# Attention scores by 32-row float32 products and a pass through DRAM, in place of split products with pre-mixed queries

## What is computed

```
x  -> group norm -> q, k (256 channels), v4 (1024 channels), each a 1x1 convolution with scale and shift
vl = 3x3 depthwise convolution of v4, scaled and shifted
attn[h,i,j] = SCALE * sum_d q[h,i,d] k[h,j,d] + ab[h, offset(i,j)]
attn = einsum('hij,gh->gij', attn, th1w) + th1b      # heads mixed
attn = softmax(attn over j)
attn = einsum('hij,gh->gij', attn, th2w) + th2b      # heads mixed again
out  = x + conv1x1(relu(attn @ v + vl))
```

## Time and profile before

| what | value |
|---|---|
| median of three runs | 4534.46 us (4534.35 to 4535.85) |
| the profiled execution's own time | 4534.58 us |
| its span, first to last instruction | 4532.8 us |
| TensorE, VectorE, ScalarE, GpSimd busy | 99%, 93%, 79%, 30% |
| granted TensorE clock, mean | 0.999 of full |
| one steady round | 70.27 us |
| DMA engines busy, mean | 27.3%, 356 MB in all |

### The profile page before, as it was taken

The page is one execution under the profiler, slowest core; times in us unless marked ns, Lnnn a source line. Parts: engine busy times, 40 slices in busy tenths (PEclk is TensorE's granted clock), DMA queues, the critical chain, the costliest instruction groups (busy, mean ns, idle before and its releaser), DMA issues.

```text
span 4532.8 us, 108461 instructions
## 1 busy us (share of the span) xinstructions
PE 4505.5 (99%) x33666; PEld 4502.5 (99%) x33666; DVE 4197.4 (93%) x10015; ACT 3570.3 (79%) x8508; POOL 1360.9 (30%) x1288
## 2 busy tenths in 40 slices
PE   7999999999999999999999999999999999999999
PEld 7999999999999999999999999999999999999999
DVE  8999999999999999999999999999999999999998
ACT  7787877878778787787787877878778778787786
POOL 2323323323233232332322323323233232332322
PEclk9999999999999999999999999999999999999999
DMA  3322222223222232222322322223222232232222
GB/s 94 97 65 81 86 69 87 65 81 92 70 81 74 72 97 65 81 82 68 93 65 81 88 72 82 68 78 97 65 81 79 67 97 65 81 86 68 88 65 76
DMA packets 211502, 356.05 MB, mean 79 GB/s; under 512 B 15843, under 2 KB 132691, under 8 KB 211413
## 3 DMA queue, kind: packets, MB, share of 16 engines
q1 hardware_dynamic: 211478, 355.75, 27.3%
HBM read 199.71 MB, written 155.98 MB: 78 GB/s over the span
## 4 chain that ended last, share of the span: by engine, by line
PE 99%; DMA 0%; POOL 0%; DVE 0%; SPq 0%; ACT 0%; issue 0%; POOLq 0%; DVEq 0%
PE psA L293 45%; PE psA L426 15%; PE psL L293 13%; PE psM L293 10%; PE psM L404 9%; PE psL L404 7%; PE psA L306 0%; DMA qa<-in_wqkv 0%; SPq L254 0%; POOL xs L822 0%; DVE probs L730 0%; DMA by_key<-probs 0%; POOL wp_lo L863 0%; DVE q_lo L722 0%; ACT w_hi L443 0%
## 5 line engine op out<-in xcount | busy, mean ns | idle before, releaser
L700 DVE SCALAR_TENSOR_TENSOR psC<-vpad,par,psC 128x406 f32<-128x406 f32 x3072 | 1807.2, 635 | 0.0
L584 ACT ACTIVATE probs<-probs,nmax 112x196 f32<-112x196 f32 x1792 | 803.2, 451 | 128.8 <-DVE nmax L759 112.9
L293 PE MATMUL psA<-x_hi,w_lo 128*128 128x392 f32 x2304 | 794.9, 345 | 6.0 <-DVE x_lo L679 6.0
L293 PE MATMUL psA<-x_hi,w_hi 128*128 128x392 f32 x2304 | 785.7, 341 | 0.0
L293 PE MATMUL psA<-x_lo,w_hi 128*128 128x392 f32 x2304 | 785.1, 341 | 0.0
L426 PE MATMUL psA<-qa,shared 105*128 105x196 f32 x4096 | 690.9, 329 | 0.0
L426 PEld LDWEIGHTS psA<-qa,shared 105*128 105x128 f32 x4096 | 677.2, 190 | 0.4 <-DVE shared L794 0.3
L857 POOL TENSOR_TENSOR k_lo<-qk,k_hi 128x392 fp32r<-128x392 f32 x128 | 159.9, 1249 | 1636.4 <-ACT k_hi L490 1636.4
L722 DVE SCALAR_TENSOR_TENSOR q_lo<-qk,th,q_hi 128x392 fp32r<-128x392 f32 x1024 | 618.3, 632 | 2.0 <-ACT q_hi L486 1.9
L486 ACT ACTIVATE q_hi<-qk,th 128x392 fp32r<-128x392 f32 x1024 | 594.5, 618 | 2.1
L461 ACT ACTIVATE o_hi<-shared 128x392 fp32r<-128x392 f32 x512 | 271.6, 530 | 391.3 <-DVE shared L794 391.3
(11 more groups left out here) (85 smaller groups left out, 10723.1 us busy)
## 6 DMA issues: line engine op xcount, KB each, us to landing
by_key<-probs SPq DMA_DIRECT2D x512, 224.0 KB, 3.6
qa<-by_key SPq DMA_DIRECT2D x128, 448.0 KB, 4.3
qk<-by_key SPq DMA_DIRECT2D x128, 448.0 KB, 6.9
xs<-in_x SPq DMA_DIRECT2D x64, 588.0 KB, 3.8
shared<-in_x SPq DMA_DIRECT2D x64, 588.0 KB, 3.8
out<-shared SPq DMA_DIRECT2D x63, 588.0 KB, 3.0
qa<-in_wqkv SPq DMA_DIRECT2D x3, 768.0 KB, 7.1
stage_wp<-in_wp SPq DMA_DIRECT2D x1, 1536.0 KB, 9.6
```

What stands on the lines that cost most here:

```text
L293: last = nc.tensor.matmul(dst, w, r, start=(begin and n == 0), stop=(end and n == 2))
L584: nc.scalar.activation(row, row, ACT.Exp, bias=nmax[:, img, b:b + 1], scale=-1.0, accum_out=rowsum[:, img, b:b + 1]).then_inc(s_exp, 1)
L700: nc.vector.scalar_tensor_tensor(a if tap == 7 else sums, src, taps[:, c, TAPS[tap]:TAPS[tap] + 1], a if tap == 0 else sums, MUL, ADD).the ...
```

## The change

Scores are made per head, unmixed, from unsplit q and k, go through DRAM, and the heads are mixed by one matmul with a Kronecker product of th1 and the identity (`kron1`) as the stationary operand.

- **q and k** stay plain float32. SCALE is folded into the scale and shift of q (setup). q's columns are stored (column w, row b) in each image. The high and low halves of q and k, `th1`, k's split on GpSimd and the tensors for them are gone.
- **TensorE, behind value tile 3**: `head_scores`, four units (image 0 or 1; the first 112 or the last 84 queries). A unit is 8 matmuls, for two halves kt of the heads and four row tiles r, on 32 partitions each; tile r has a PSUM bank of its own out of psL and psM.
- **Copies**: ScalarE copies banks 0 and 1 of each unit, VectorE banks 2 and 3, into `scores` (part of `qa`). Each unit but the first waits for all four copies of the one before.
- **SyncE**: 8 stores of the scores to `head_rows` (two per unit, 784 B runs), then one load per image into `by_head` (112 partitions (head, column), 14 x 196 numbers each, part of `shared`), all ahead of the stores of turned values. The turned values' loads now wait for their stores alone. The row of ones is loaded once.
- **TensorE, logits**: behind projection 0, now 14 matmuls of 392 columns, one per two query rows. Projection 1 moves behind the logits.
- **VectorE**: 16 convolution steps, score copies, 8 steps, the turns (after three units' stores have landed), 4 steps, the 28 score rows with no convolution steps between them, then 18 steps before the second reciprocal.
- **ScalarE**: q and k right behind each other; value tiles 4 to 7 behind the score copies; the output of projection 1 is taken between exponentials 20 and 21.

```diff
+            def head_scores(t, first):
+                pe.wait_ge(s_qk_sb, 4 * t + 4)
+                for u, (img, c) in enumerate(UNITS):
+                    if u:
+                        pe.wait_ge(s_score_a, 8 * t + 2 * u)
+                        pe.wait_ge(s_score_v, 8 * t + 2 * u)
+                    elif not first:
+                        pe.wait_ge(s_mix_sb, 14 * t)
+                    at_ = img * PIX + c * WIDE
+                    for kt in range(QT):
+                        for r in range(QUADS):
+                            part_ = slice(r * KD, (r + 1) * KD)
+                            mm = nc.tensor.matmul(score_bank(r)[0:score_rows(c), kt * PIX:(kt + 1) * PIX],
+                                                  q[part_, kt, at_:at_ + score_rows(c)],
+                                                  k[part_, kt, img * PIX:(img + 1) * PIX], start=True, stop=True)
+                    mm.then_inc(s_score_mm, 1)
...
+                    if m == 3:
+                        head_scores(t, first)
...
                     project(t, 0, True)
-                    project(t, 1, True)
-                pe.wait_ge(s_klo, 2 * (t + 1))
-                pe.wait_ge(s_qlo, 16 * (t + 1))
                 for n in range(RES):
                     img, b0 = n // 7, 2 * (n % 7)
+                    if n % 7 == 0:
+                        pe.wait_ge(s_heads[img], 16 * (t + 1))
                     if n >= 4:
                         pe.wait_ge(s_score, 28 * t + 2 * n - 6)
...
+                    nc.tensor.matmul(logit_bank(n)[:, 0:2 * PIX], kron1[:, :, :].rearrange("p g i -> p (g i)"),
+                                     by_head[:, img, b0 * PIX:(b0 + 2) * PIX], start=True, stop=True
+                                     ).then_inc(s_logit_mm, 1)
...
+                    project(t, 1, True)
...
+            def score_copy(t, u, r):
+                img, c = UNITS[u]
+                act.wait_ge(s_score_mm, 4 * t + u + 1)
+                nc.scalar.copy(scores[0:score_rows(c), img, c, r:NH:QUADS, :],
+                               score_bank(r)[0:score_rows(c), :].rearrange("p (k n) -> p k n", k=QT)
+                               ).then_inc(s_score_a, 1)
...
+            def scores_out(t, u):
+                img, c = UNITS[u]
+                sp.wait_ge(s_score_a, 8 * t + 2 * u + 2)
+                sp.wait_ge(s_score_v, 8 * t + 2 * u + 2)
+                rows = head_rows[img].rearrange("h i j -> i h j")
+                middle = 4 * 16 if c == 0 else REST - REST % 16
+                parts = [(0, middle), (middle, score_rows(c))]
+                for lo, hi in parts:
+                    sp.dma_start(rows[c * WIDE + lo:c * WIDE + hi], scores[lo:hi, img, c, :, :]
+                                 ).then_inc(s_score_out[u], 16)
...
-                convs(6)
-                for _ in range(8):
-                    mixed_low(1)
-                    convs(1)
...
+                convs(16)
+                score_copies()
+                convs(8)
+                for u in range(3):
+                    dve.wait_ge(s_score_out[u], 32 * (t + 1))
                 turn(0)
...
                 turn(1)
...
-                convs(6)
+                convs(4)
                 for n in range(RES):
...
-                    convs(1)
-                convs(3)
+                convs(18)
```

More of the change, by code:

```diff
@@ L231, in _ @@
                 sp.dma_start(stage_w[:, :, cols], w_rows[:, :, cols]).then_inc(s_w[n], 16)
-            for dst, src in ((par[:, :], A["par"]), (th1[:, :, :], A["th1"]), (small[:, :], A["small"]),
+            for dst, src in ((par[:, :], A["par"]), (small[:, :], A["small"]),
                              (abx[:, :], A["abx"]),
@@ L274, in step @@
                     load_x(t + 1)
+                for u in range(4):
+                    scores_out(t, u)
+                if first:
+                    sp.wait_ge(s_bias, 1)
+                else:
+                    sp.wait_ge(s_olo, 8 * t)
+                    wait_alone(sp, s_av_mm, 8 * t)
+                heads_in(t, 0)
+                heads_in(t, 1)
                 turned_out(t)
-                ones_in(t)
                 keys_in(t)
@@ L390, in step @@
                 if not first:
+                    if not last:
+                        pe.wait_ge(s_gs, t + 2)
+                    project(t, 1, True)
+                if not first:
                     project(t, 2, True)
-                pe.wait_ge(s_ones_in, 16 * (t + 2))
+                if first:
+                    pe.wait_ge(s_ones_in, 16)
                 for use, (img, n) in enumerate(USES):
@@ L532, in step @@
                 conv_centre(t, 1)
+                if not first:
+                    act.wait_ge(s_vt_sb, 4 * t)
+                query_or_key(0)
+                query_or_key(1)
+                query_or_key(2)
+                query_or_key(3)
+                values(2)
+                values(3)
                 if first:
@@ L590, in step @@
                         conv_centre(t, CENTRES[n])
+                    if n == 20 and not first:
+                        projected(t, 1)
                 if not first:
@@ L595, in step @@
                     act.wait_ge(s_mix_mm, 14 * t + use + 1)
-                    if use == 0 and not first:
-                        act.wait_ge(s_av_mm, 8 * t)
+                    if use == 0:
+                        act.wait_ge(s_vt_out, OUTS * (t + 1))
                     if use == 7:
@@ L714, in step, with score_copies @@
                     dve.wait_ge(s_av_mm, 8 * t)
[L715 to L723 removed]
+                def score_copies():
+                    if first:
+                        dve.wait_ge(s_wlo, CT)
+                    else:
+                        dve.wait_ge(s_vt_sb, 4 * t)
+                    for u, (img, c) in enumerate(UNITS):
+                        dve.wait_ge(s_score_mm, 4 * t + u + 1)
+                        for r in (2, 3):
+                            nc.vector.tensor_copy(scores[0:score_rows(c), img, c, r:NH:QUADS, :],
+                                                  score_bank(r)[0:score_rows(c), :].rearrange("p (k n) -> p k n", k=QT)
+                                                  ).then_inc(s_score_v, 1)
                 def turn(half):
@@ L854, in step @@
             def step(t, first, last):
-                for kt in range(QT):
-                    wait_alone(pool, s_khi, 2 * t + kt + 1)
-                    nc.gpsimd.tensor_tensor(k_lo[:, kt, :], k[:, kt, :], k_hi[:, kt, :].bitcast(f32),
-                                            SUB).then_inc(s_klo, 1)
                 if first:
```

149 lines of the change are left out of this document (47 added, 102 removed).

## The result

The changed kernel takes 5054.52 us (median of four runs, 5048.46 to 5068.05), the kernel before 4535.01 on the same chip: a ratio of 1.115, with a 95% interval of 1.1124 to 1.1175. It is slower by 520 us. The forecast said slower by 296 (4830, range 4600 to 5150): the direction and the range held, the point was 225 us low. The profiled execution took 5059.76.

A forecast was written before the change was run, and what follows sets the result against it. TensorE was taken to bound the kernel end to end. A round: 12.85 + 10.6 + 10.7 + 9.45 + 8.6 + 10.75 + 10.63 + 1.3 = 74.9 us against 70.27, over 64 rounds 296 more: 4830 us, range 4600 to 5150.

The forecast's parts named there:

- What bounds the kernel before; slower, since each wait of TensorE is added in full: Whole round: TensorE's instructions set its 70.27 us, any TensorE wait adds in full; slower had chance 0.93.
- Scores, 10.6 us: Four score units on TensorE: three turns of 3.05 us plus 1.5, in place of nothing.
- the 1.5 us of passes in a unit: TensorE's 16 score passes per unit: 1.5 us taken, between 0.66 (four tiles at once) and 2.66 (one after the other).
- the first rival: Score units: row tiles overlap fully, units 0.66, turns about 2.3, scores 7.7, round 72.0, 4646 us; chance 0.2.
- VectorE's copies, forecast at 1.06: Between score units: two copies of 392-column banks, 0.49 + 0.57 = 1.06 us, with 1.3 as the upper case.
- Through DRAM, "I cost them at nothing": Score stores and head-row loads: both images' rows land just before TensorE asks, 0.5 to 1 us in hand, no cost.
- VectorE, a stall of 1.3 at the value product: Value product's third group, nominally at 42.15, waits for VectorE's first addition, done at 43.45: 1.3 us a round.
- "nothing, without reserve": Image 1's mixing weights: ready at 34.2 us and wanted at 34.2, so no wait.
- The clock, a rival at 0.1: Scores: TensorE's clock falls, as it is idle for half of some 10 us there; chance 0.1.
- The sum again: Whole round: terms add to 74.9 us against 70.27, 4.63 x 64 = 296 us more, 4830 us.
- Checks of "what the profile after would show": Profile after: TensorE some 92% busy, three copy waits a round of some 1.6 us, score passes about 0.17 apart, DMA near half.
- Two of the three signs of "wrong": Signs: score passes under 0.1 or over 0.3 apart; head-row wait over 1 us; 392-column matmuls behind scores 0.33 apart.

The follow-up runs named there:

- f3_row_order: Changed kernel with the two loops of a score unit exchanged, both matmuls of a row tile issued one behind the other: 5069.67 us, ratio 1.1191.
- g1_filler: Changed kernel plus six matmuls of 392 columns, results unread, behind each of the first three score units: 5007.33 us, ratio 1.1033.
- f4_heads_ready: Changed kernel with head rows loaded from x at the round's start, scores stored but unused: 4917.57 us in one execution, 5051.8 to 5055.9 in three.
- h3_turn_late: Changed kernel reordered: score units spread, image 0's load before the last two units' stores, value transposes behind image 0's row minima, turned-row copies later: 4670.01 us, ratio 1.0297.

## Why the prediction was right, and where it was not

- **What bounds the kernel before; slower, since each wait of TensorE is added in full**: right. TensorE's instructions fell, its idle time did more than make up for it.
- **Scores, 10.6 us**: wrong by 3.2 us a round, 205 us too much. The term that failed is the 1.5 us of passes in a unit, which no run shows: in after and in f3_row_order the passes start four at a time, one of each row tile, the groups 0.25, 0.17 and 0.17 us apart, so a unit has some 0.66 us of passes (4 x 0.166), and the order of the loops makes no difference. That a matmul is two passes did not stand in the way. The turn was 2.17: the first rival had this, with 7.7 for the scores against 7.4 (by the forecast's own terms it would be 3 x 2.22 + 0.66 = 7.3). Counted from the first start to the last end, a unit takes 0.93 us where the 16 passes one after the other would take some 2.8 (an estimate, 15 x 0.166 + 0.33), three times as long. VectorE's copies, forecast at 1.06, took 1.04.
- **Through DRAM, "I cost them at nothing"**: wrong by 109 us, and by some 220 were the clock full above it. The packets were priced well (52 ns against 50). Two things went wrong. Eight stores held SyncE for 10.63 us, so that image 0's load is issued 6 us behind the last unit's passes and image 1's 9, and a load took 8.9 us from issue, 9.0 in the median, where the sum had 4.2 of packets and up to 2.7 for the rest. So image 0's rows land 21.5 us after the first unit's start, where the forecast's times give 20.2 to 20.9. And TensorE asks for them at 18.3 in place of 21.3, since the scores are 3.2 shorter: that is the larger part. Time won in the scores was lost again at the head rows.
- **VectorE, a stall of 1.3 at the value product**: the mechanism was right, the size 1.9 (39 us more). The mixing weights, "nothing, without reserve", cost 28.
- **The clock, a rival at 0.1 against "each gap is under 1.6 us"**: it came, with 228 us, of which I had none. The reason against it failed: with gaps of 1.24 us between the units the scores' end or the tiles behind it run at a granted clock of 0.50 in 48 of 63 rounds, and g1_filler, which fills the gaps, takes that away (none of 63). The waits for VectorE and for the DMA have half clock behind them too. As measured this is the largest term of the miss; but some 110 us of it hide a wait of the same length.
- **The sum again**: 4830 - 205 + 109 + 39 + 28 + 224 (228 less the 4 of before) = 5025. The 35 that are left to 5060 are mostly one line: value tiles 4 to 7 and projection 0 take 11.05 in place of 10.7 at full clock, 22 us (the second matmul starts 0.28 behind the first in place of 0.18, and the last one's 0.34 has nothing to overlap with). So the point was out by 225 because errors of 400 and 205 stood against each other; the range held partly by that.
- **Checks of "what the profile after would show"**: copy waits three a round (1.24, said 1.6), passes 0.17 apart, TensorE near 92% (90), DMA near half (47%) are right. Two of the three signs of "wrong" came true: the head-row wait is over 1 us a round, and matmuls of 392 columns behind the scores come 0.33 apart in some rounds.

What stays open is why the half clock came in 48 rounds behind the scores and not in the other 15, and what set one of the four executions of f4_heads_ready apart. Not tried: staging the scores in memory that the transposes don't use, and a second DMA queue for the loads; both would have needed a rewrite of the memory plan or of an engine's order.

## What to carry to other kernels

A kernel that is bound by one engine from end to end is best read in three terms: its instructions at full clock, its idle time, the half clock. A change that trades instructions for hand-offs (points where one engine must wait for another's result) must be priced by all three, and here 194 us of instructions saved cost 720 of the other two. When an operand goes through DRAM, count the time that the queue is held by what stands ahead of the load and its whole time from issue to landing, not its bytes alone. The terms can't be added up one by one, either: here a stretch at half clock ahead of the wait for the head rows cost nothing by itself (20.1 us in place of 18.3 on the way there, the logits at 21.7 either way), and shorter work ahead of bytes that came at their own time brought nothing. And a wait that is removed shows its worth only when the next one is known: the same move (the head-row load earlier) was worth minus 101 us with the transposes ahead of the row minima, and together with their move (and that of ScalarE's copies) plus 76.

## What the runs showed of the hardware

- Four plain float32 row tiles of 32 rows run fully side by side: 16 passes of 196 columns start in groups of four, 0.17 us apart (the second group 0.25), in either order of the loops, and are through in 0.93 us.
- Short idle stretches can cost the clock: with three waits of 1.24 us in 7.4 us the granted clock fell to 0.50 in or behind them in 48 of 63 rounds, and with matmuls in these waits in none. At 5058 us of span, 228 us were lost to the half clock, and 10 in a program (h3_turn_late) that still idled 289 us in waits of mostly 0.8 to 1.5 us, the longest behind its first round 2.1.
- Executions of one program (f4_heads_ready) were 2.8% apart, with a mean clock of 0.935 and 0.975.
- Eight stores of 24.5 to 490 KB, in packets of 784 B, held SyncE for 0.6 to 2.1 us each; a load of 1.2 MB behind them took 9.0 us from issue to landing (median).
- Work for nothing can pay: 18 idle-filling matmuls a round, 241 us of them, made the program 47 us faster.
- Four instructions of a round moved within VectorE's program gave 178 us, 81 of them the wait that they were aimed at.
